# A fused convolution and deformable convolution kernel: offset stage reordered, part of it moved into the sampling loop, folds to nine slots, a shorter end

## What is computed

```python
# block 1: two 3x3 branches, each times a sigmoid attention map: x = x + _L0_conv_ref(_gn(x), ...)
# block 2: x = x + _L1_conv_ref(_gn(x), ...), of which:
offs = _conv3x3(x, offset_w, offset_b).reshape(Nb, KK, 2, Hh, Ww)
off_y, off_x = (offs[:, :, 0], offs[:, :, 1])
mask = 2.0 * jax.nn.sigmoid(_conv3x3(x, mod_w, mod_b))
...
sy = off_y + hy[None, None, :, None] + kyy[None, :, None, None]
sx = off_x + wx[None, None, None, :] + kxx[None, :, None, None]
...
sampled = jax.vmap(per_img)(x, sy, sx).reshape(Nb, C, KK, Hh, Ww)
sampled = sampled * mask[:, None]
w = weight.reshape(C_OUT, C, KK)
out = jnp.einsum('nckhw,ock->nohw', sampled, w) + bias[None, :, None, None]
mean = out.mean(axis=(0, 2, 3), keepdims=True)
var = ((out - mean) ** 2).mean(axis=(0, 2, 3), keepdims=True)
out = (out - mean) * jax.lax.rsqrt(var + BN_EPS)
out = out * gamma[None, :, None, None] + beta[None, :, None, None]
return jax.nn.relu(out)
```

## Time and profile before

| | us |
|---|---|
| runs shown: median (lowest to highest) | 366.09 (365.16 to 371.99) |
| profiled execution, its own time | 368.4 |
| its span, first to last instruction | 366.6 |
| mean granted TensorE clock, share of full | 0.912 |
| busy in the span: PE, DVE, ACT, POOL | 271.8, 278.5, 239.0, 237.7 |
| first multiplication of the loop (L1241) starts at | 123.3 |
| last sum of the loop (L1249) starts at | 330.7 |

### The profile page before, as it was taken

One profiled execution on the slowest core, in us unless ns is written; L12 is line 12 of the kernel. 1 busy time (PEld: TensorE's weight loads), 2 busy tenths in 40 slices (PEclk: granted clock), 3 DMA queues, 4 the chain that ended last, 5 costly groups with the idle time before them and its releaser, 6 DMA issues.

```text
span 366.6 us, 16294 instructions
## 1 busy us (share of the span) xinstructions
PE 271.8 (74%) x7279; PEld 192.3 (52%) x7280; DVE 278.5 (76%) x507; ACT 239.0 (65%) x340; POOL 237.7 (65%) x182
## 2 busy tenths in 40 slices
PE   0479978699564779898988888888899887633540
PEld 0448413365142556576666666666666666523540
DVE  4851489818638879979999999999999999861376
ACT  1021474108438579779999999999999988722346
POOL 9000036917106279889999999999999999993000
PEclk9989999899965699989999999999999999995565
DMA  8880000000401300200000020000002000000006
GB/s 251 166 170 18 4 0 1 2 12 20 80 0 29 74 2 7 98 36 4 4 4 6 4 100 36 4 4 6 4 13 91 36 4 5 4 22 3 0 0 229
DMA packets 11749, 14.21 MB, mean 39 GB/s; under 512 B 4247, under 2 KB 7640, under 8 KB 11644
## 3 DMA queue, kind: packets, MB, share of 16 engines
q1 hardware_dynamic: 10218, 11.53, 10.9%
q10 hardware_dynamic: 1382, 1.04, 1.3%
q0 software_dynamic: 80, 0.61, 0.9%
HBM read 4.62 MB, written 2.98 MB: 21 GB/s over the span
## 4 chain that ended last, share of the span: by engine, by line
DVE 35%; POOL 29%; PE 18%; issue 6%; DMA 5%; ACT 4%; SPq 2%; POOLq 1%; DVEq 1%; ACTq 0%
POOL prod L505 17%; DVE prod L1241 17%; POOL prod L509 9%; PE ps L537 6%; DVE areg L1249 5%; PE ps L618 3%; DMA x_sb<-in_x 2%; DVE wreg L1145 2%; DVE x_sb L1325 2%; PE ps L548 1%; DMA hy<-xpad 1%; DVE prod L1107 1%; PE ps L723 1%; PE ps L636 1%; PE ps L798 1%
## 5 line engine op out<-in xcount | busy, mean ns | idle before, releaser
L723 PE MATMUL ps<-zreg,hx 64*64 64x96 f32 x4608 | 129.7, 253 | 25.6 <-DVE prod L1241 23.7
L1241 DVE TENSOR_TENSOR prod<-ps,hy 128x480 f32<-128x480 f32 (+1 forms) x256 | 138.0, 601 | 9.4 <-PE ps L723 3.4
L723 PEld LDWEIGHTS ps<-zreg,hx 64*64 64x64 f32 x4608 | 114.8, 136 | 45.7 <-ACT hx L955 30.1
L505 POOL TENSOR_TENSOR prod<-prod 128x832 f32<-128x832 f32 x64 | 125.8, 1965 | 15.5 <-DVE prod L1241 13.0
L878 ACT ACTIVATE hx<-ps 128x576 f32<-128x576 f32 x131 | 78.1, 648 | 34.9 <-PE ps L636 14.8
L955 ACT ACTIVATE hx<-hx,rbias 128x1152 f32<-128x1152 f32 x64 | 81.0, 1265 | 0.7
L509 POOL TENSOR_TENSOR prod<-prod 128x384 f32<-128x384 f32 x64 | 66.4, 1037 | 5.0
L1249 DVE TENSOR_REDUCE areg<-prod 128x64 f32<-128x512 f32 x64 | 44.5, 695 | 13.8 <-POOL prod L509 11.4
L636 PE MATMUL ps<-wz,xpad 32*64 32x144 f32 (+1 forms) x1024 | 35.2, 330 | 7.6 <-issue 4.0
L469 POOL TENSOR_TENSOR x_sb<-prod,x_sb 128x512 f32<-128x512 f32 x8 | 10.6, 1333 | 46.1 <-DVE prod L1107 46.1
L951 ACT ACTIVATE zreg<-ps 128x576 f32<-128x576 f32 x56 | 36.9, 659 | 0.0
(11 more groups left out here) (154 smaller groups left out, 285.7 us busy)
## 6 DMA issues: line engine op xcount, KB each, us to landing
zreg<-zreg SPq DMA_DIRECT2D x12, 288.0 KB, 2.3
out<-x_sb SPq DMA_DIRECT2D x8, 256.0 KB, 2.1
x_sb<-in_x SPq DMA_DIRECT2D x3, 512.0 KB, 4.8
preg<-scratch SPq DMA_DIRECT2D x16, 54.0 KB
zreg<-in_pos POOLq DMA_DIRECT2D x1, 528.0 KB, 5.7
x_sb<-in_x SPq DMA_DIRECT2D x2, 256.0 KB, 7.2
scratch<-prod SPq DMA_DIRECT2D x12, 36.0 KB
scratch<-zreg SPq DMA_DIRECT2D x12, 36.0 KB
```

The lines of the kernel that those rows point to most:

```text
L505: pool.tensor_tensor(slots[:, :, 0:2 * moved], slots[:, :, 0:2 * moved], slots[:, :, 2 * KEPT:6 * KK], ALU.add).then_inc(half_folded, 1)
L723: return pe.matmul(g_ps(g, h)[u * W:(u + 1) * W, k - TAPS[h][0], :, :], hx[s, (t + u) % 4, k, :], z_sb[s, b, at:at + 3, k * C:(k + 1) * C] ...
L1241: mul = vector.tensor_tensor(pv[:, n0:n1], gv, wv[:, n0:n1], ALU.mult)
```

## The change

1. **Sigmoid in place.** ACT writes the sigmoid back to the PSUM bank, and DVE multiplies from there. `map_chunk` now waits for DVE's multiplication (`sig_used`).
2. **Constants of `px`.** The clearing of `preg` by POOL is gone; five small transfers fill the constant rows.
3. **Leads.** `norm2` comes in six pieces. Leads 0 to 5 are made ahead of and between the taps of the first step, in banks 4 to 7; leads 6 and 7 between those of the second. ACT saves 0, 2, 4, 7 and DVE 1, 3, 5, 6.
4. **First step's split.** ACT writes the high part from PSUM (`save_high`), DVE subtracts it from PSUM (`split_bank`, two instructions of 256 an image), and only then ACT saves `offc`. The parts are laid out without the stride that they had.
5. **Two queues.** Of the first step's transfers, 2 stores of the low part and 4 of the 8 loads are issued by ACT.
6. **Second step.** Its parts have room of their own (`parts1`), so ACT's wait for `px_ready[1]` in iteration 2 is gone. `turn_step(1)` comes behind the first distances; DVE saves its offsets. The last two low parts, the reach reductions and the vertical weights of the second step (ACT's four instructions, DVE's nine) stand in iterations 0 to 12 of the loop.
7. **Folds.** POOL folds 14 to 9 slots (5 x 64 elements an instruction instead of 6 x 64), DVE adds up 9.
8. **End.** PE's `far_rows` no longer waits for the last sum; of the 12 rows to stage, 8 go to ACT and 4 stay on POOL, and PE starts with ACT's. All 8 chunks get PSUM banks of their own, statistics and the last activation read PSUM, one product gives mean and second moment together. The last stage begins with two half chunks. The search for far offsets stands at iterations 15 to 17.

The core of the diff:

```diff
-SUMMED = 8
+SUMMED = 9
-        REACH_TURN = 8
+        REACH_TURN = 15
...
             for s in range(STEPS):
                 for b in range(B + 1):
-                    if b < B:
+                    if b < B and s > 0:
                         pool.wait_ge(cv_saved, B * s + b + 1)
...
-            conv2_taps(0, range(KK)).then_inc(cv_ready, 1)
...
+            lead(0)
             pe.wait_ge(norm2, 4)
+            for n, t0, t1 in ((1, 0, 1), (2, 1, 3), (3, 3, 5), (4, 5, 7), (5, 7, 8)):
+                conv2_taps(0, range(t0, t1))
+                lead(n)
+            conv2_taps(0, range(8, KK)).then_inc(cv_ready, 1)
...
-                act.activation(sig[:, u, :], ps[:, (2 + u) * BANK:(3 + u) * BANK], ACT.Sigmoid)\
-                    .then_inc(sig_ready, 1)
+                act.activation(ps[:, (2 + u) * BANK:(3 + u) * BANK], ps[:, (2 + u) * BANK:(3 + u) * BANK],
+                               ACT.Sigmoid).then_inc(sig_ready, 1)
...
+            act.wait_ge(parts_ready, B)
+            for j in range(2, SPREAD):
+                store_part(act, 0, NPART - 1, j)
+            for n in range(4):
+                vertical(0, n)
+            act.wait_ge(parts_stored, 16 * SPREAD * NPART)
+            for j in range(SPREAD):
+                load_px(act, 0, j, 1)
+            save_lead(ACT_LEADS[3])
...
-                if i == 2:
-
-                    act.wait_ge(px_ready[1], 16 * PX_DMAS)
...
+                if 3 <= i < 7:
+                    vertical(1, i - 3)
...
+            def split_bank(b):
+
+                vector.wait_ge(high_ready, b + 1)
+                for u in range(2):
+                    half = slice(u * BANK // 2, (u + 1) * BANK // 2)
+                    ins = vector.scalar_tensor_tensor(
+                        rest[0][b][:, half].rearrange("p (r x) -> p r x", x=W),
+                        rows_of(ps[:, b * BANK:(b + 1) * BANK])[:, :, u, :], offbc[:, :],
+                        parts[0][:, 0, b, half].rearrange("p (r x) -> p r x", x=W), ALU.add, ALU.subtract)
+                ins.then_inc(rest_ready, 1)
...
             for i in range(NT // 2):
                 weigh(i, 0)
                 weigh(i, 1)
+                if i < 2:
+                    split_low(1, i + 2)
+                elif i < 4:
+                    reaches(i - 2)
+                elif 4 <= i < 13:
+                    r, part_of = (i - 4) // 3, (i - 4) % 3
+                    if part_of < 2:
+                        vertical_weights(1, 2 * r + part_of)
+                    else:
+                        vertical_rest(1, r)
                 if i > 0:
                     add_up(i - 1)
...
+                stage_rows(act, lambda to, of: act.activation(to, of, ACT.Copy), FAR_HIGH, y, row)\
+                    .then_inc(far_staged_high, 1)
...
-            pe.wait_ge(acc_ready, NT)
-
             pe.wait_ge(reach_ready, 2)
             far_rows(pe, far_tile, far_turn)
...
+            pe.matmul(ps[:, 0:2], avg4[:, :], small[:, MVB:MVB + 2], start=True, stop=True).then_inc(bmean_ready, 1)
...
-                vector.wait_ge(outt_saved, c + 1)
-                vector.bn_stats(bstats[:, c, :], out_t[:, c * BANK:(c + 1) * BANK]).then_inc(st_ready, 1)
+                vector.wait_ge(outt_made, c + 1)
+                vector.bn_stats(bstats[:, c, :], ps[:, c * BANK:(c + 1) * BANK]).then_inc(st_ready, 1)
```

364 lines of the change are left out of this document (194 added, 170 removed).

## The result

The changed kernel takes **346.84 us** in the median (344.90 to 348.12, 4 runs), the kernel before beside it 368.36 (365.16 to 371.99): a ratio of **0.9439 [0.9326, 0.9552]**. Applied to the 366.1 against which the sum was made, that is 345.6. The forecast was 350.1 with a range of 343.5 to 360.0. Ratios and their intervals use the fast runs alone, and as the profiled executions of a_fold8 and b_sig were slow ones, only single instructions and stretches are read from these two.

The account below looks back on a forecast made before the run. The prediction took the loop to be bound by a ring of fold, sum and multiplication, not by one engine's work. Its terms -2.7 + 0.1 - 12.4 + 6.0 - 2.0 - 5.0 = -16.0 took 366.1 to 350.1 us, range 343.5 to 360.

Parts of the forecast that it names:

- ring of three links: In the loop: POOL's fold 3.1, sum 0.8 and multiplication 2.25 us, run twice over in turn, set the pace.
- 1. Sigmoid in place: First block: DVE's product read from PSUM costs 0.75 us instead of 1.37; -2.7 us, bounds 0 and -3.2.
- POOL's own addition of 1.27 holds it at about 1.36: First block: the step from chunk to chunk falls from 1.92 to about 1.36 us, held there by POOL.
- 2. First tap to fourth multiplication: Ahead of the loop and into it: first multiplication at 38 instead of 51.3, fourth at 50 instead of 62.4; -12.4 us.
- the half clock that was charged: Ahead of the loop: after idling 3 us for the loads, PE's transposes, distances and taps run at clock 0.50.
- 3. Extras in the loop: Iterations 3 to 12: added DVE instructions cost 5.3 us and ACT's four 0.7; +6.0 us, bounds 2.5 and 14.
- the pair is lost each time: Rival for the loop: POOL wins the shared ports at each of six products, +9, low parts +2; 361 us, chance 0.15.
- 4. Nine slots: Loop: the fold saves 0.13 us, DVE's sum costs about 0.08 more, 0.025 an iteration; -2.0 us in all.
- 5. The end: Behind the last sum: staging -3.0, statistics -1.0, aggregation to activation -0.75, half chunk -0.3; -5.0 us, bounds -3 and -6.
- the first case: Whole kernel: the steps hold as forecast, with errors of 4 or so; 346 to 354.5 us, chance 0.55.
- more comes free: Rival: loop extras fall into slack and PE's clock stays up ahead of and into the loop; 342.3 us, chance 0.13.
- Leads cost what they gain: Rival ahead of the loop: later loads, 5 us of transfers restarted by two queues, slow PE iterations; 356 us, chance 0.12.

Follow-up runs that it names:

- a_fold8: The changed kernel with eight fold slots again instead of nine: 352.86 us, ratio 0.9584 to the kernel before.
- b_sig: The kernel before with the sigmoid in place and nothing else: 364.22 us, ratio 0.9906 to the kernel before.
- b_fold9: The kernel before with nine fold slots instead of eight and nothing else: 361.79 us, ratio 0.9840 to the kernel before.
- a_end_pool: The changed kernel with ten of the twelve staged far rows on POOL and two on ACT: 350.04 us, ratio 0.9560 to the kernel before.
- a_ahead: The changed kernel with the second step's vertical weights and two reductions ahead of the loop again: 348.99 us, ratio 0.9499 to the kernel before.
- a_probe: The changed kernel with one unread 288-element DVE instruction added per iteration in three stretches of six loop iterations: 358.32 us, run once.
- a_leads_late: The changed kernel with the eight leads behind the first step's convolution again, their copies behind that step's splits: 354.98 us, ratio 0.9714 to the kernel before.
- a_one_queue: The changed kernel with all transfers of the first step issued by SP: 346.02 us, ratio 0.9432 to the kernel before.
- a_fold10: The changed kernel with ten fold slots instead of nine: 347.45 us, ratio 0.9445 to the kernel before.

## Why the prediction was right

**What bounds it.** The ring of three links held for the loop of the kernel before: b_fold9 shortened one link, and each pair of iterations by 0.19. In the changed kernel both bounds stand close together, ring and DVE, which is why ten slots (DVE +0.065, POOL -0.024) are worse than nine.

**1. Sigmoid in place, forecast -2.7, measured -1.65** from the third product to N. The product is 0.75 as said. The step that failed is "POOL's own addition of 1.27 holds it at about 1.36": it left out that the sigmoid now occupies PE's bank until the product is done. The pace is the ring PE, ACT, DVE, 1.655 on average, and that mean holds two steps slowed by a clock of 0.50 (2.16 and 1.71); the two at full clock average 1.38, as forecast. That all of the excess would be gone at full clock is argued from these steps and not shown by a run.

**2. First tap to fourth multiplication, forecast -12.4, measured -13.9.** Its parts: high parts begin at 14.1 behind the first tap (13.5), parts done 21.1 (20.6), loads issued 25.4 (24.1), landed 32.0 (30, at the upper bound), first multiplication 38.1 (38), fourth 48.4 (50). The landing came 2 later than forecast, and the half clock that was charged did not occur: from landing to the first multiplication it took 6.1 instead of 7.7. In the profiled execution these cancel, so that 38.1 against 38 is luck. In a_end_pool, where the clock did fall, the two come 40.1 and 50.7 behind the first tap. The forecast of the clock was thus right for a part of the executions and wrong for the profiled one. The prediction had DVE's last four subtractions end together with PE's taps; the windows show DVE as close to the bound from the second step's splits on (2.97 of 3.00 ahead of 102), which it did not say.

**3. Extras in the loop, forecast +6.0, measured +4.1** (a_ahead). The order of events was right: DVE's product goes first and POOL waits. The size was not: I charged each extra in full to POOL's fold in the ring, but DVE is full in these iterations (3.40 against 3.02), and POOL idles 0.3 to 0.8 ahead of each fold, which takes up its wait. The charge is an extra's own length less DVE's slack of 0.2 (0.57 and 0.38, 0.74 and 0.56). The case "the pair is lost each time" priced such a wait at 1.5 on top of this; a_probe measured 1.13 on top where the order is turned round, and none of the ten iterations turned it. Of the two low parts, which the prediction put under PE's slow iterations, one met a fold (0.6 longer, iteration 1).

**4. Nine slots, forecast -2.0, measured -6.2 and -6.9 in the traces.** The failed step is "2.1 ns an element, so 64 elements less save 0.13". It drew a line through folds of 832 and 384 elements; between 384 and 320 it is 0.246. The rows of before held the two sizes only, so the price should have been a range. This is the largest miss of the sum. About 1.1 of it is the half clock in the three iterations of the search, which had no term at all and is not shown to come from the folds.

**5. The end, forecast -5.0, measured -5.06,** by other parts than said: far product -3.7 (forecast -3.0), statistics -0.4 (-1.0, since the transposes took 6.43 and not 5.97), aggregation to activation -1.0 (-0.75), half chunk 0 (-0.3).

**The sum.** Errors of +1.1 in step 1, -1.5 in 2, -1.9 in 3, -4.5 in 4, -0.1 in 5 and -0.6 ahead of the third product and of the first tap leave the profiled span 7.5 below the forecast. Taken off 366.1 as the forecast was, the span's -23.5 would give 342.6, below the stated range. The median lies only 3.3 below the forecast, in the first case's range of 346 to 354.5, because the profiled execution of before took 368.4 and not 366.1, and that of the changed kernel was the shortest of its four. So the mechanisms of four steps held, two sizes were well off in the same direction (3 and 4), and that the median came so close is partly luck. Of the rivals "more comes free" named both things that did (smaller extras, a clock that stays up, at least sometimes) but not the fold. "Leads cost what they gain" is refuted by a_leads_late, and its other half, that two queues start the transfers' 5 us again, by a_one_queue: one queue or two, 6.5 us.

## What to carry to other kernels

An instruction's price by size is not to be interpolated between two sizes far apart: on POOL one slot less was worth 0.25 and the next 0.02, and a kernel is well served by timing each size once. An instruction with two SBUF inputs is cheap on DVE straight behind an event that also releases POOL, and waits for the rest of POOL's instruction if it comes a little later (0.45 became 1.77), so its place in the order matters more than its length. And where work is moved out of a late stretch into a loop, ask which engine has no gap in both places: here it was DVE in both, and what was gained was only the 2 us of DVE's slack in the loop (6.0 against 4.1). Last, before a difference between two traces is put down to an edit, compare the granted clock of the two stretches: here a lower clock goes with the slow steps of step 1 and with about 1.1 of step 4.

## What the runs showed of the hardware that was not expected

- POOL's addition of two SBUF tiles over 832, 384, 320 and 256 elements took 1.97, 1.037, 0.791 and 0.767 us, that is 2.4, 2.7, 2.5 and 3.0 ns an element.
- DVE with two SBUF inputs beside POOL's fold: the second waits for the first to end, in both orders (0.45 becoming 1.77 on DVE; 1.97 becoming 2.11 to 2.2 on POOL). Behind an instruction with one SBUF input the fold was 2.25 at most (L1220), behind a reduction with one it was 1.96 to 1.97. The Trainium skill (page "SBUF — State Buffer", section "SBUF: two separate sides") says that who starts first holds the shared ports; in the loop that was DVE in iterations 2 to 12, with 0.16 or 0.17 between the two starts, and POOL, by 0.08, in iteration 1.
- Behind the same pause of 3 us PE's clock stayed at 1.00 in one profiled execution (the changed kernel), stood at 0.50 for some 3 us in two (a_probe, a_one_queue) and for some 10 in three (a_fold8, a_fold10, a_end_pool).
- With the sigmoid in place PE's clock stood at 0.50 for some 3 us of the first block in 11 of 11 kernels, without it in 0 of 3; in the search for far offsets it did so in 3 of 4 with eight slots and in 0 of 10 with more.
- Eight loads of 54 KB landed 6.5 to 6.6 us behind the first issue, from one queue or from two.
